# Two running-state attentions: another order of the state products, and the reciprocal in PSUM

## The reference

```
layer 0:  q, k = elu(.)+1                          layer 1:  q, k rotated and scaled by the decay
S_t = S_(t-1) + k_t v_t^T ;  z_t = z_(t-1) + k_t   S the same, no z
num[j] = sum_i q[i] S_t[i, j] ;  den = sum_i q[i] z_t[i]
y = num / (den + 1e-6)                             y = (out - mean) * rsqrt(var + 1e-5)
```

## Time and profile before

| what | value |
|---|---|
| median of 3 runs | 1319.41 us (1318.48 to 1320.2) |
| the profiled execution | 1326.37 us, its span 1324.6 us |
| first attention | from about 60 to 410 us of the span |
| second attention | from about 510 to 825 us |
| busy over the whole span | DVE 79%, PE 75%, POOL 64%, ACT 45% |
| line 455, kv on POOL | 268.3 us in 128 instructions |
| line 559, halving on POOL | 173.9 us in 128 |
| line 573, sum on DVE | 165.2 us in 128 |
| line 613, y on DVE | 129.2 us in 128, mean 1009 ns |
| line 543, products on DVE | 180.1 us in 384 |

### The profile page before, as it was taken

One profiled execution on the slowest core, in us unless ns is written; L12 is line 12 of the kernel. 1 busy time (PEld: TensorE's weight loads), 2 busy tenths in 40 slices (PEclk: granted clock), 3 DMA queues, 4 the chain that ended last, 5 costly groups with the idle time before them and its releaser, 6 DMA issues. The chain is left out here.

```text
span 1324.6 us, 25269 instructions
## 1 busy us (share of the span) xinstructions
PE 989.8 (75%) x5489; PEld 687.1 (52%) x5489; DVE 1050.3 (79%) x2728; ACT 598.7 (45%) x1554; POOL 851.1 (64%) x728
## 2 busy tenths in 40 slices
PE   4788888888876867888887885378876777777774
PEld 3444444444444644444444543255656676666663
DVE  3599999999995976999999997557665595777775
ACT  1543434344325955656656543266536402333331
POOL 0366666666662217988888885767834306888885
PEclk9799999999996988999999998579985557999998
DMA  6500000000000021000000000523442203323331
GB/s 193 166 3 0 0 0 0 0 0 0 0 1 0 0 84 45 16 8 16 16 8 16 16 9 16 144 72 98 103 104 78 72 1 89 88 88 89 92 90 31
DMA packets 67118, 61.25 MB, mean 46 GB/s; under 512 B 7813, under 2 KB 54097, under 8 KB 67043
## 3 DMA queue, kind: packets, MB, share of 16 engines
q1 hardware_dynamic: 58978, 41.47, 11.3%
q0 software_dynamic: 6912, 18.36, 4.8%
q10 hardware_dynamic: 1152, 0.52, 0.1%
HBM read 30.97 MB, written 21.50 MB: 40 GB/s over the span
## 5 line engine op out<-in xcount | busy, mean ns | idle before, releaser
L464 PE MATMUL a_pS<-a_kv,utri 128*128 128x360 f32 (+3 forms) x768 | 271.3, 491 | 16.4 <-DVE a_tt L543 11.6
L559 POOL TENSOR_TENSOR a_tt<-a_tt 128x576 f32<-128x576 f32 (+1 forms) x128 | 173.9, 1359 | 162.8 <-DVE a_tt L543 161.3
L455 POOL TENSOR_TENSOR a_kv<-a_qk,a_vv 128x1152 f32<-128x1152 f32 (+1 forms) x128 | 268.3, 2097 | 13.2 <-DVE a_qk L429 13.2
L464 PEld LDWEIGHTS a_pS<-a_kv,utri 128*128 128x128 f32 x768 | 139.9, 196 | 99.4 <-DVE a_tt L543 30.8
L543 DVE TENSOR_TENSOR a_tt<-a_pS,a_qk 128x360 f32<-128x360 f32 (+3 forms) x384 | 180.1, 521 | 10.1 <-PE a_pS L464 10.1
L573 DVE TENSOR_REDUCE a_nd<-a_tt 128x144 f32<-128x720 f32 (+3 forms) x128 | 165.2, 1290 | 0.0
L613 DVE TENSOR_TENSOR a_y<-a_nd,a_rec 128x128 f32<-128x128 f32 x128 | 129.2, 1009 | 2.5 <-issue 0.2
L1766 POOL DMA_INDIRECT x_yl<-ys,e_row x72 | 70.3, 976 | 68.2 <-POOLq L1479 53.9
L509 ACT ACTIVATE a_tt<-a_pI 128x144 f32<-128x144 f32 (+1 forms) x96 | 27.7, 289 | 141.7 <-PE a_pI L472 141.7
L1772 POOL DMA_INDIRECT out_dram<-x_o,e_row_z x72 | 73.3, 1017 | 25.2 <-DVE x_o L1760 20.8
L1694 ACT ACTIVATE x_hT<-x_pA,x_w 128x128 f32<-128x128 f32 x144 | 45.1, 364 | 89.8 <-PE x_pB L1686 87.3
(11 more groups left out here) (260 smaller groups left out, 2440.9 us busy)
## 6 DMA issues: line engine op xcount, KB each, us to landing
ys<-gw SPq DMA_DIRECT2D x16, 256.0 KB, 3.7
xs<-X SPq DMA_DIRECT2D x16, 256.0 KB, 2.3
X<-xs SPq DMA_DIRECT2D x16, 256.0 KB, 5.5
m_kx<-m_kc SPq DMA_DIRECT2D x64, 64.0 KB, 2.0
ys<-X SPq DMA_DIRECT2D x16, 256.0 KB, 3.2
m_ax<-m_pc SPq DMA_DIRECT2D x64, 64.0 KB, 2.0
ys<-U SPq DMA_DIRECT2D x16, 256.0 KB
w<-in_L_ffn_W_dram SPq DMA_DIRECT2D x1, 2048.0 KB, 12.0
```

The source lines that it names most:

```text
L455: pool.tensor_tensor(kv[:, t % 2, :, :, :], kk.unsqueeze(3).to_broadcast([P, H, D, J]), vv[:, t, :, :].unsqueeze(2).to_broadcast([P, H, D, ...
L464: pe.matmul(pS[c][:, 0:(h1 - h0) * SC], K.utri[:, :], flat[:, h0 * SC:h1 * SC], start=True, stop=True).then_inc(u_done, 1)
L559: pool.tensor_tensor(tt[:, t % 2, 0:HH, D // 2:D, :], tt[:, t % 2, 0:HH, D // 2:D, :], tt[:, t % 2, 0:HH, 0:D // 2, :], ALU.add).then_inc( ...
```

## The change

The same sums are computed in another layout. `kv` and `tt` go from head, row, column to head, column, row: `kv` is [16, J, 8], `tt` is [16, J, 9], so the numbers that are summed for one output are neighbours in memory, and each group of them starts 9 elements behind the last. The inner run of POOL's kv product goes from J to 8 and that of the halving from 4·J to 4; the run that DVE's products write goes from 8·J to 8; ACT's row D becomes single elements 9 apart; `vec_sum` becomes a reduction over five (in the first tile of a batch four) neighbours. `rec` is no tile of SBUF any more but 16 columns of the PSUM bank `pO`, which the output projection also writes; so `pe_project` of tile m now also waits until y of tile m+1 is made. In layer 0 the reciprocal moves behind the residual, as in layer 1, and at the end of each layer one residual goes ahead of the last reciprocal. The case in which fewer than three banks are halved is dropped; it was not in use.

```
-        kv = sb("kv", [P, 2, H, D, J])
-        tt = sb("tt", [P, 2, H, D + 1, J])
+        kv = sb("kv", [P, 2, H, J, D])
+        tt = sb("tt", [P, 2, H, J, D + 1])
-        rec = sb("rec", [P, H])
+        rec = pO[:, 256:256 + H]
...
-            pool.tensor_tensor(kv[:, t % 2, :, :, :], kk.unsqueeze(3).to_broadcast([P, H, D, J]),
-                               vv[:, t, :, :].unsqueeze(2).to_broadcast([P, H, D, J]), ALU.mult).then_inc(kv_ready, 1)
+            pool.tensor_tensor(kv[:, t % 2, :, :, :], kk.unsqueeze(2).to_broadcast([P, H, J, D]),
+                               vv[:, t, :, :].unsqueeze(3).to_broadcast([P, H, J, D]), ALU.mult).then_inc(kv_ready, 1)
...
             wait(pe, x_done, m)
+            pe.wait_ge(y_ready, NT if isinstance(b, int) and m == NT - 1 else m + 2)
             pe.matmul(pO[:, 0:P], yT[:, :], tile(K.wgate[:, 0 if layer == 0 else 2, :, :], b),
...
-            act.activation(tt[:, t % 2, :, D, :], pI[:, P:P + H * J].rearrange("p (h j) -> p h j", h=H),
+            act.activation(tt[:, t % 2, :, :, D], pI[:, P:P + H * J].rearrange("p (h j) -> p h j", h=H),
...
-                v.tensor_tensor(tt[:, t % 2, h0:h1, 0:D, :],
-                                pS[c][:, 0:(h1 - h0) * SC].rearrange("p (h i j) -> p h i j", i=D, j=J),
-                                q[:, h0:h1, :].unsqueeze(3).to_broadcast([P, h1 - h0, D, J]),
+                v.tensor_tensor(tt[:, t % 2, h0:h1, :, 0:D],
+                                pS[c][:, 0:(h1 - h0) * SC].rearrange("p (h j i) -> p h j i", i=D, j=J),
+                                q[:, h0:h1, :].unsqueeze(2).to_broadcast([P, h1 - h0, J, D]),
                                 ALU.mult).then_inc(t_done, 1)
...
-            pool.tensor_tensor(tt[:, t % 2, 0:HH, D // 2:D, :], tt[:, t % 2, 0:HH, D // 2:D, :],
-                               tt[:, t % 2, 0:HH, 0:D // 2, :], ALU.add).then_inc(half_done, 1)
+            pool.tensor_tensor(tt[:, t % 2, :, :, D // 2:D], tt[:, t % 2, :, :, D // 2:D],
+                               tt[:, t % 2, :, :, 0:D // 2], ALU.add).then_inc(half_done, 1)
...
-            for h0, h1, first in ((0, HH, D // 2), (HH, H, 0)):
-                if h0 < h1:
-                    red = v.tensor_reduce(nd[:, t % 2, h0:h1, :], tt[:, t % 2, h0:h1, first:rows, :]
-                                          .rearrange("p h i j -> p h j i"), AX.X, ALU.add)
-            red.then_inc(red_done, 1)
+            v.tensor_reduce(nd[:, t % 2, :, :], tt[:, t % 2, :, :, D // 2:rows], AX.X, ALU.add).then_inc(red_done, 1)
...
                     if layer == 1:
                         vec_var(v, 4 * before[0] + before[1])
-                    else:
-                        vec_rec(v, 4 * before[0] + before[1])
...
                 if before:
-                    if layer == 1:
-                        vec_rec(v, 4 * before[0] + before[1])
+                    vec_rec(v, 4 * before[0] + before[1])
                     vec_y(v, 4 * before[0] + before[1], before[1])
```

More of the change, by code:

```diff
@@ L289, in attention @@
     heads = [(0, 6), (6, 11), (11, 16)]
-    banks_halved = 3
-    HH = heads[banks_halved - 1][1]
     sh, scl = (SA0, CA0) if layer == 0 else (SA1, CA1)
@@ L460, in pe_states @@
             pe.wait_ge(kv_ready, n + 1)
-            flat = kv[:, t % 2, :, :, :].rearrange("p h i j -> p (h i j)")
+            flat = kv[:, t % 2, :, :, :].rearrange("p h j i -> p (h j i)")
             for c, (h0, h1) in enumerate(heads):
@@ L557, in pool_halve @@
             n = 4 * b + t
-            pool.wait_ge(t_done, 3 * n + banks_halved)
-            pool.tensor_tensor(tt[:, t % 2, 0:HH, D // 2:D, :], tt[:, t % 2, 0:HH, D // 2:D, :],
-                               tt[:, t % 2, 0:HH, 0:D // 2, :], ALU.add).then_inc(half_done, 1)
+            pool.wait_ge(t_done, 3 * n + 3)
+            pool.tensor_tensor(tt[:, t % 2, :, :, D // 2:D], tt[:, t % 2, :, :, D // 2:D],
+                               tt[:, t % 2, :, :, 0:D // 2], ALU.add).then_inc(half_done, 1)
         def vec_sum(v, b, t):
@@ L604, in vec_rec @@
                 v.wait_ge(den_done, n + 1)
-                v.reciprocal(rec[:, :], den[:, :]).then_inc(rec_done, 1)
+                v.reciprocal(rec, den[:, :]).then_inc(rec_done, 1)
             else:
                 v.wait_ge(sd_done, n + 1)
-                v.reciprocal(rec[:, :], sd[:, :]).then_inc(rec_done, 1)
+                v.reciprocal(rec, sd[:, :]).then_inc(rec_done, 1)
         def vec_y(v, n, t):
@@ L613, in vec_y @@
             v.tensor_tensor(y[:, :].rearrange("p (h j) -> p h j", h=H), nd[:, t % 2, :, 0:D],
-                            rec[:, :].unsqueeze(2).to_broadcast([P, H, D]), ALU.mult).then_inc(y_ready, 1)
+                            rec.unsqueeze(2).to_broadcast([P, H, D]), ALU.mult).then_inc(y_ready, 1)
         def vec_residual(v, b, t):
@@ L783, in _ @@
                     vec_var(v, NT - 1)
+                vec_residual(v, B - 1, 1)
                 vec_rec(v, NT - 1)
                 vec_y(v, NT - 1, 3)
-                for t in (1, 2, 3):
+                for t in (2, 3):
                     vec_residual(v, B - 1, t)
```

## The result

The changed kernel takes 1196.8 us (median of 4 runs, 1192.7 to 1201.1) against 1319.8 us for the kernel before in the same session: a ratio of 0.906, with a 95% interval of 0.901 to 0.911. It was forecast to be faster, at 1235 with a range of 1206 to 1292.

What follows compares the result with a forecast made beforehand. A DVE-POOL loop, with y held behind kv, bounded the first attention; POOL was almost full in the second. Savings of 60 and 24 us, together 84, took the profiled 1326.4 to 1242; less 7.0, 1235 us, range 1206 to 1292.

Steps and rivals of the forecast that it cites:

- The loops: Both attentions: y, freed of POOL's kv, leaves 2.83 us plus halving h a tile in the first; POOL bounds the second.
- The halving: POOL's line 559, in runs of 4: dearer by 0.20 and 0.18 us, so h = 1.63 and 1.46 us.
- rival A: Halving on POOL no dearer; PE's floor binds the first attention, POOL the second: 1220 us, about 1210 at low h; chance 0.20.
- The low bound: Halving on POOL: at best 0.25 us below today's, from 1038 ns for 512 numbers against 1286 for the halving.
- PE's floor: PE's busy time as least time a tile: 4.45 us in the first attention, 3.97 in the second.
- The sum: DVE's sum over neighbours: 1.0 us instead of 1.43; gain covered in the first attention, off the path in the second.
- PE's new wait: Projection of tile m waiting for y of m+1: costs nothing, as the wait should already be over.
- The margins for bounds that lie near each other: Tile periods rounded up for imperfect overlap: first attention 4.46 to 4.5 us, second 4.53 to 4.6.
- B: Halving on POOL half dearer, h = 2.15 and 1.93 us: 1290 us; chance 0.12.
- D: POOL pays by the run in line 559, halving at twice the time, 2.86 and 2.57 us: slower, 1376 us; chance 0.06.
- E: y on DVE isn't freed, because reading `nd` holds it; only the dearer halving counts: 1343 us; chance 0.03.
- C: PE keeps gaps of half a microsecond a tile on top of its busy time: 1277 us; chance 0.12.

## Why the prediction was wrong in size

**The loops.** Right. y lost its hold (286 to 289 ns over all 128), den was held to the end of the halving, and the period of the first attention came out as 2.83 + h: with the measured h of 1.28 that is 4.11, and it was 4.06. The second attention became POOL's, as said, at 4.14 us in three tiles of a batch; the tile that waits for the root takes 4.95, and the mean is 4.29.

**The halving.** This step failed, and it is a term of both loops. It was forecast to rise by 0.20 and 0.18 us and fell by 0.15 and 0.12. 0.35 us over 63 tiles are 22 us in the first attention and 0.30 are 19 in the second: 41 us, where 39 are missing. Alone it doesn't close the gap: with the right halving the prediction's own sum would still have stopped the first attention at PE's 4.45, as rival A did, and only the second attention's 19 us would have come. The 22 need the next step too. The price of the short runs, derived from POOL's kv rows, was right where it was measured by itself with far inputs (0.20 us). What was left out was that the two inputs come to lie near each other, which at this pitch takes off 0.32. The low bound, from the 1038 ns that line 100 takes for 512 numbers, had the size but not the reason: the two inputs of that row lie in two tiles, and both are repeated. Why it is cheap was not asked, and no run here shows it.

**PE's floor.** This step failed too, and it is why the range was too narrow. 4.45 us busy a tile was read as the least that PE needs. After the change PE was busy 15.38/4 = 3.85 us a tile for the same work, and the experiment with den on ACT shows 3.51 in a tile. PE in the first attention before the change:

```profile
218.46 2.20 PE L464 MATMUL a_pS<-a_kv,utri 128*128 128x432 f32 x6
220.65 0.48 PE L472 MATMUL a_pI<-a_R,a_qT 128*128 128x144 f32 x2
220.97 0.41 PE L479 MATMUL a_pR<-a_vv,a_qk 128*128 128x144 f32 x2
221.45 0.88 PE L392 MATMUL a_pQ<-wqkv,a_hT 128*128 128x384 f32 x2
```

The rows are as long as those of the experiment with den on ACT or little longer, but there the next one starts before the last has ended: 1.93 us from the states to the next row, then 0.25 and 0.25, where before the change it is 2.19, 0.32 and 0.48. Rows of PE overlap when it goes straight on, and a short pause between two of them vanishes inside a row that counts as busy. So the 4.45 held pauses. What each pause waited for was not traced. Without that floor, rival A at the low bound of h would have been 2.83 + 1.18 = 4.01 us in the first attention, 28 us below the 4.45 that it was priced with, near 1182, and the range would have held the result.

**The sum.** 0.89 us, where 1.0 was taken with 0.90 as the bound; the odd starts cost nothing. That its gain would be covered in the first attention held for the layout alone, where den and y took it. It didn't hold for the change: with the reciprocal in PSUM and the old sum the first attention was at 4.72 us, not 4.26, since DVE's own work is then 4.36 and den was held by kv in nine tiles. The prediction named the hold at its end as what would make it wrong, and didn't see that the short sum prevents it: no den took over 0.77 us in the changed kernel. In the second attention the sum was said to be off the path; with the old sum DVE, not POOL, is the bound there, and the tile that waits for the root stays at 5.83.

**The small ones.** kv was 0.07 us cheaper in the first attention (2.17 against 2.24; 0.05 was the bound). The products 0.52 and 0.60 us as before. The reciprocal written to PSUM 0.24 us as before. ACT's scattered row 0.43 us against 0.30, nearly the 0.15 more that was the bound, and hidden. PE's new wait: in the first attention PE waited 7.7 us in all for y there, 0.3 us at most, and has room for it. The margins for bounds that lie near each other (0.04 us in the first attention, 0.07 in the second) were not needed in the first.

**Rivals.** The time is nearest to A, below its low end, and its condition, a halving no dearer, was met and more. B and D, a dearer halving, fell with the measured 1.28 us, E with y's 0.29. C, gaps of PE on top of 4.45, fell with tiles of 4.06 us. Of the Trainium skill's rule in B, that reads with steps over 8 bytes cost half as much again, no run shows anything, as each input has a step of one element inside its runs. The rule on 8-byte starts ("Vector Engine (DVE) Microarchitecture Reference" of the Trainium skill, "Measured stream behaviour on trn2") gives more time for pairs from odd words; for the sum's runs of five with a pitch of 9 no extra time was measured, 0.92 us both ways. The rule on the shared port ("SBUF — State Buffer" of the Trainium skill, "Who interferes with whom") agrees with these runs, and it also covers den, whose form, by that section, can enter a mode with two ports: 1.75 us beside POOL with an SBUF end and 0.19 with a PSUM end.

## What to carry to other kernels

An instruction whose duration varies fivefold is waiting inside itself: find what the other engine runs at that moment, and move one operand or the result to PSUM. Follow the period round its loop before adding up savings; a part that is hidden behind a wait today can pay in full once that wait is gone, so two edits can be worth more together than the sum of both alone. Busy time of PE that is read where it keeps pausing is no lower bound; and when a layout changes, ask not only for the length of the runs but also how far apart an instruction's two inputs come to lie.

## What the runs showed of the hardware that I had not expected

- POOL, 576 sums of plain neighbours in fp32: 1.19 us with inputs 1 to 5 elements apart, 1.44 with 7 or more, or in two tiles (neither input repeated). Runs of 4 take 1.32 with a pitch of 9 at distances 4 and 5, 1.44 and 1.45 with a pitch of 8 and 10 at distance 4, and 1.64 with a pitch of 9 and the second input in another tile.
- The addition of DVE to 16 numbers with both ends in SBUF (den) can be held like a large operation: 1.75 to 2.23 us beside a product of POOL, against 0.15 to 0.18 us free, and 0.17 to 0.19 with its result in PSUM. The reciprocal of 16 numbers, also within SBUF, took 0.25 us beside the same products.
- A DVE sum over runs of five that start at every ninth element is as fast as a dense one: 0.92 us for 720 numbers, against 1.44 in single steps.
